# Delta stage's opening: the gate projection over four array quarters with its weights held, and the first convolutions between the normalizations

## The chip, the cores and the metric

One NeuronCore of a Trainium2 chip runs the whole program. The metric is the device time of one execution in microseconds. The profiled execution is another one, taken with the hardware profiler on.

## What is computed

The kernel is a decoder of two layers with six sub-layers (A to F): delta attention, cross attention, a mixture of experts with two choices, local attention, cross attention, and a mixture of 32 experts. Each adds to x. The change lies in the first, A, whose reference begins so (B = 2 sequences of T = 1024 tokens, 256 features, H = 4 heads, NH = 2 key steps a token):

```python
q = short_conv(hidden_states @ Wq, wq_conv).reshape(B, T, H, DK)
k = short_conv(hidden_states @ Wk, wk_conv).reshape(B, T, NH, H, DK)
v = short_conv(hidden_states @ Wv, wv_conv).reshape(B, T, NH, H, DV)
q = l2norm(q)
k = l2norm(k)
beta = 2.0 * jax.nn.sigmoid(hidden_states @ Wb).reshape(B, T, NH, H)
g = -jnp.exp(A_log) * jax.nn.softplus(hidden_states @ Wa + dt_bias)
```

hidden_states is the layer-normalized x; short_conv is a causal convolution over 4 tokens for each channel, and silu. Behind it comes a recurrence over the tokens, which the kernel does in 32 chunks of 32 tokens.

## The kernel before

Every engine runs its own queue in order, and a list `order`, written out in `stage_a`, sets for all of them in which order the steps stand. Each engine's function walks the list and issues its part of a step; semaphores tie the parts together. A step that waits holds everything behind it on its engine.

The steps of the opening:

- **stat, norm, ln** (eight times, for pairs of token tiles in the order `halves`): statistics on DVE (L262, L265), the root on POOL (L284 and `newton`), the normalization on DVE (L275), four transposes on PE (L296), a copy into `XT` on ACT (L304). DVE does stat i two turns ahead of norm i.
- **z**: the projection to the twelve gate columns (Wb and Wa) on PE, L594. Tokens are the stationary operand: 64 matmuls (two passes each) hold 64 tokens and move 12 columns.
- **gates 0, 1, 2**: the gates on DVE and ACT, with small matmuls between 1 and 2 (L604 to L610). **rows** turns the summed decays and sends them to memory (`decays`, `grown`), from where they come back spread over all partitions into `a_E` and `KQg`.
- **conv n, c** (here n = 0, the first 128 tokens, 16 channel tiles c): matmuls on PE (L582, two of 128x256), two copies on ACT (L929, L930), three multiply-adds on DVE (L782). The banks 2, 3, 4 and 7 are taken in turn. On all three engines it waits until `w_in` counts all eight loads of the stage, which SP issues behind x and the constants. **silu** is on ACT (L949), with a small copy on POOL (L1043).
- **kt, sq, root, small, decay**: transposes and norms of the keys, then the decay matrices. From ("kt", 0, 0) on, the chain over the chunks begins.

The order before puts all eight normalizations first, then z and gates 0, then the convolutions:

```python
order += [("z",), ("gates", 0)] + conv0[0:4] + [("gates", 1)] + conv0[4:7] + [("gates", 2), ("rows",)] + conv0[7:11] + silu0[0:4]
```

Of the kernel before, what the change touches and what calls it, by code (L numbers as in the profile page):

```python
# [14 lines left out]
ACT = mybir.ActivationFunctionType  # L15
AX = mybir.AxisListType.X

P = 128
B, T, D = 2, 1024, 256
NT = B * T // P  # L20
TB = T // P
KD = D // P
# [6 lines left out]
R = P // B  # L29
# [109 lines left out]
def program(nc, a, out, stages="ABCDEF"):  # L139
    _, at, _, _ = constant_arrays()  # L140
    with ExitStack() as ctx:
# [20 lines left out]
        XT = sb("XT", [P, KD, B * T])  # L162
# [4 lines left out]
        ident, ones = const("ident"), const("ones")  # L167
# [139 lines left out]
        def stage_a(sx):  # L307
            t_ = lambda name, shape, dt=F32: sb("a_" + name, shape, dt, ctx=sx)
            wqkv, lo = weight_view("a_wqkv", wa, 0)
            wba, lo = weight_view("a_wba", wa, lo)  # L310
# [50 lines left out]
            CP = NC // 2  # L361
            spare_e = E[1][:].rearrange("p a h r -> p (a h r)")
            z = spare_e[:, 0:192].rearrange("p (c n) -> p c n", n=12)
            za, g = (spare_e[:, q:q + CP * H].rearrange("p (c h) -> p c h", h=H) for q in (192, 256))
            n0, n1 = (spare_e[:, q:q + NC * H].rearrange("p (e c h) -> p e c h", e=2, h=H) for q in (384, 512))
# [31 lines left out]
            conv0 = [("conv", 0, q) for q in tiles]  # L397
            silu0 = [("silu", 0, q) for q in tiles]
            halves = [0, 4, 1, 5, 2, 6, 3, 7]
            order = []  # L400
            for i in range(len(halves) + 2):
                order += [("stat", "A", n2) for n2 in halves[i:i + 1]]
                order += [(what, "A", halves[i - 2]) for what in ("norm", "ln")] * (i > 1)
            order += [("z",), ("gates", 0)] + conv0[0:4] + [("gates", 1)] + conv0[4:7] + [("gates", 2), ("rows",)] + conv0[7:11] + silu0[0:4]
            for i in range(11, NCH):
# [51 lines left out]
            at = {}  # L457
            for s in order:
# [6 lines left out]
                elif what == "silu":  # L465
                    silu_done.mark(*s[1:])
                    if s[1] < NB - 1:
                        history.mark(s[1] + 1, s[2])
                elif what == "z":
                    i = 5  # L470
                elif what == "gates":
# [96 lines left out]
            def tensor(t):  # L568
                for s in order:
# [15 lines left out]
                    elif what == "z":  # L585
# [3 lines left out]
                        free(t, *s)  # L589
                        for c in range(CP):  # L590
                            for j in range(KD):
                                for bb in range(B):
                                    first = bb * T + c * R
                                    i = t.e.matmul(b.ap[both(bb), c * 12:c * 12 + 12], XT[:, j, first:first + R], wba[:, j, :],  # L594
                                                   start=j == 0, stop=j == KD - 1, tile_position=(0, bb * R), skip_group_check=True)
                        i.then_inc(b.filled, 1)
# [170 lines left out]
            def vector(v):  # L767
                par = const("par")
                for s in order:
# [18 lines left out]
                    elif what == "gates":  # L788
                        beta, zz = z[:, :, 0:2 * H], z[:, :, 2 * H:3 * H]
                        over = lambda x: x[:, :].unsqueeze(1).broadcast_to([P, CP, H])  # L790
                        if s[1] == 0:
                            zb = at["z",]
                            v.wait_ge(w_in, 128)
                            filled(v, "z")
                            v.e.tensor_copy(z, zb.ap[:, 0:192].rearrange("p (u n) -> p u n", n=12)).then_inc(zb.emptied, 1)
                            emptied(v, "z")
                            v.step(v.e.tensor_tensor(zz, zz, over(dtb), ALU.add)); v.settle()
# [117 lines left out]
            def scalar(c):  # L915
                fence(c, "A")
                for s in order:
# [13 lines left out]
                    elif what == "silu":  # L931
# [16 lines left out]
                        for bb in range(B):  # L948
                            i = c.e.activation(dst[:, :, bb, :], acc_[:, :, bb, :], ACT.Silu)  # L949
                        i.then_inc(silu_done.sem, 1)  # L950
                    elif what == "gates" and s[1] == 0:
                        beta = z[:, :, 0:2 * H]
# [1855 lines left out]
def lay_out(i):  # L2808
# [3 lines left out]
    o["a_wqkv"] = np.concatenate([i["L0_attn_Wq"], i["L0_attn_Wk"], i["L0_attn_Wv"]], 1)  # L2812
    o["a_wba"] = np.concatenate([i["L0_attn_Wb"], i["L0_attn_Wa"]], 1)
    o["a_wg"], o["a_wo"] = i["L0_attn_Wg"], i["L0_attn_Wo"]
# [50 lines left out]
```

## Time and profile before

| what | before |
|---|---|
| median of three runs | 2614.67 us (2614.16 to 2616.9) |
| the profiled execution's own time | 2616.09 us |
| its span | 2614.3 us |
| PE busy | 2287.6 us, 88% |
| DVE busy | 1641.1 us, 63% |
| ACT busy | 1163.2 us, 44% |
| mean granted clock | 0.941 |

Busy time is that of the whole program; the opening spoken of here is its first 77 us. A "pass" is one matmul instruction of the trace; a 32-bit matmul of the code is two of them. Names as `a_kn` are the program's buffers.

### The profile page before, as it was taken

The page shows a single profiled execution, that of the slowest core. Times are in us where ns is not written, and L with a number is a line of the kernel's source. Part 1 is how long each engine was busy: PE and PEld are TensorE (multiplying, and loading weights), DVE is VectorE, ACT ScalarE, POOL GpSimd, SP SyncE. Part 2 cuts the span into 40 slices and gives each one's busy share as a digit, 9 for nine tenths or more (in the row PEclk, how much of TensorE's full clock was granted, in tenths as well). Part 3 has the DMA queues.
Part 4 walks back from the last instruction along what each step waited for, and adds up shares of the span by engine and source line. Part 5 has one row for each costly group of instructions (what it writes and reads, how often), then busy time and mean ns, then how long its engine had stood idle before and what let it go on. Part 6 is the DMA issues. An engine that isn't in the chain of part 4 may idle for free. (4 is left out here: it accounts for less than half of the span.)

```text
span 2614.3 us, 62054 instructions
## 1 busy us (share of the span) xinstructions
PE 2287.6 (88%) x25731; PEld 1873.6 (72%) x25731; DVE 1641.1 (63%) x3593; ACT 1163.2 (44%) x3232; POOL 735.1 (28%) x876
## 2 busy tenths in 40 slices
PE   5689989999898999964998589988887799999998
PEld 4477777777785777743887366666665688888887
DVE  4566676667644555546784455556775767767776
ACT  2544444443423554521554356656775233333332
POOL 2334243423323333331565433420011001111110
PEclk8699999999999999976999799999998899999999
DMA  3101010100103000020442300000000000000000
GB/s 100 57 10 35 27 35 10 35 27 13 61 3 108 9 18 13 13 82 17 114 124 34 103 2 2 2 2 2 2 2 14 13 25 25 25 25 25 25 7 33
DMA packets 87961, 83.35 MB, mean 32 GB/s; under 512 B 27264, under 2 KB 83456, under 8 KB 86272
## 3 DMA queue, kind: packets, MB, share of 16 engines
q1 hardware_dynamic: 81536, 70.98, 8.7%
q0 software_dynamic: 6144, 8.39, 1.9%
q8 instruction: 204, 3.34, 0.5%
q14 instruction: 77, 0.63, 0.1%
HBM read 68.71 MB, written 10.65 MB: 30 GB/s over the span
## 5 line engine op out<-in xcount | busy, mean ns | idle before, releaser
L2566 PE MATMUL bank<-f_XH,f_wp 128*128 128x512 f32 x1088 | 365.4, 397 | 5.9 <-issue 4.5
L782 DVE SCALAR_TENSOR_TENSOR a_acc<-a_praw,a_convw,a_acc 128x256 f32<-128x256 f32 x345 | 205.4, 596 | 99.4 <-ACT a_acc L930 91.2
L2566 PEld LDWEIGHTS bank<-f_XH,f_wp 128*128 128x128 f32 x1088 | 209.1, 192 | 48.5 <-issue 4.9
L2566 PEld LDWEIGHTS bank<-f_wp,f_Hp 128*128 128x128 f32 x1632 | 215.0, 192 | 28.6 <-DVE X L2703 17.0
L2566 PE MATMUL bank<-f_wp,f_Hp 128*128 128x256 f32 x1632 | 219.3, 284 | 17.2 <-DVE X L2703 16.3
L2566 PE MATMUL bank<-f_XL,f_wp 128*128 128x512 f32 x544 | 216.6, 398 | 0.0
L2701 DVE SCALAR_TENSOR_TENSOR X<-bank,f_w,X 128x256 f32<-128x256 f32 x512 | 211.4, 476 | 0.0
L2750 POOL TENSOR_TENSOR f_wp<-wa,f_wp 128x768 fp32r<-128x768 f32 x34 | 62.8, 1848 | 526.2 <-ACT f_wp L2716 526.2
L2739 ACT ACTIVATE f_Hp<-f_H 128x512 fp32r<-128x512 f32 x136 | 85.9, 632 | 225.9 <-DVE f_H L2688 225.9
L582 PE MATMUL bank<-XT,wa 128*128 128x256 f32 x512 | 160.5, 446 | 7.6 <-ACT a_acc L930 6.6
L2737 ACT ACTIVATE f_G<-bank 128x512 f32<-128x512 f32 x136 | 81.3, 598 | 166.0 <-PE bank L2566 166.0
L2690 DVE TENSOR_TENSOR f_Hp<-f_H,f_Hp 128x512 fp32r<-128x512 f32 x136 | 94.2, 692 | 94.9 <-ACT f_Hp L2739 94.9
L669 PE MATMUL bank<-wa 64*64 64x64 f32 x2560 | 108.5, 230 | 46.4 <-DVE wa L871 32.8
L2688 DVE TENSOR_TENSOR f_H<-bank,f_G 128x512 f32<-128x512 f32 x136 | 94.0, 692 | 82.1 <-PE bank L2566 82.1
L2044 DVE TENSOR_REDUCE d_mx<-bank 128x2 f32<-128x512 f32 (+1 forms) x128 | 75.2, 650 | 106.6 <-PE bank L1979 106.6
L669 PEld LDWEIGHTS bank<-wa 64*64 64x64 f32 x2560 | 89.6, 140 | 70.6 <-DVE wa L871 43.6
L997 ACT ACTIVATE wa<-bank 128x256 f32<-128x256 f32 x160 | 58.4, 386 | 159.5 <-PE bank L669 158.7
L1395 POOL TENSOR_TENSOR b_P<-b_P,b_rec 128x616 f32<-128x616 f32 x64 | 77.6, 1212 | 182.9 <-DVE b_rec L1333 182.9
L2114 ACT ACTIVATE d_P<-bank,d_mx 128x256 f32<-128x256 f32 (+1 forms) x256 | 95.1, 479 | 74.6 <-DVE d_mx L2044 74.6
L582 PEld LDWEIGHTS bank<-XT,wa 128*128 128x128 f32 x512 | 100.0, 215 | 28.3 <-ACT a_acc L930 8.9
L2566 PEld LDWEIGHTS bank<-f_XL,f_wp 128*128 128x128 f32 x544 | 104.8, 193 | 16.9
L2432 ACT ACTIVATE e_P<-e_P,e_mx 128x154 f32<-128x154 f32 x256 | 90.7, 415 | 50.2 <-DVE e_mx L2383 50.2
(370 smaller groups left out, 5439.2 us busy)
## 6 DMA issues: line engine op xcount, KB each, us to landing
wa<-in_c_w SPq DMA_DIRECT2D x64, 256.0 KB, 3.3
wa<-in_f_gu SPq DMA_DIRECT2D x34, 256.0 KB, 2.8
wb<-grown SPq DMA_DIRECT2D x4, 1536.0 KB, 6.8
a_KQg<-grown SPq DMA_DIRECT2D x4, 1536.0 KB, 6.6
wa<-in_f_d SPq DMA_DIRECT2D x34, 128.0 KB, 2.9
a_E<-decays SPq DMA_DIRECT2D x16, 256.0 KB, 4.0
X<-in_x SPq DMA_DIRECT2D x4, 512.0 KB, 5.3
wa<-in_a_wqkv SPq DMA_DIRECT2D x1, 2048.0 KB, 11.9
```

The lines of the kernel that those rows point to most:

```text
L582: i = t.e.matmul(b.ap[:, 0:B * BT_].rearrange("p (b t) -> p b t", b=B), wqkv[:, j, c * P:(c + 1) * P], xt, start=j == 0, stop=j == KD - 1, ...
L669: i = t.e.matmul(heads(b.ap)[both(bb), h, :], nt[c % 2][both(bb), h, :], xx[c % 2][both(bb), 0, h, :], start=True, stop=True, tile_positio ...
L782: i = v.e.scalar_tensor_tensor(A_, praw[:, c, :, j:j + BT_], convw[:, c, j:j + 1], A_, ALU.mult, ALU.add)
L1395: g.e.tensor_tensor(p_, p_, bc(rec[:, u % NPB].rearrange("p a b -> p (a b)"), S2), ALU.mult).then_inc(scaled.sem, 1)
L2114: i = c.e.activation(Pm[of(g, r)][:, j, lo:], pair(b.ap)[:, j, lo:], ACT.Exp, bias=mx[:, of(g, r), j:j + 1])
L2432: i = c.e.activation(p_[:, j, :], p_[:, j, :], ACT.Exp, bias=mx[:, of(g, r), j:j + 1])
L2566: i = t.e.matmul(out_, lhsT[x], rhs[y], start=n == 0 and k == 0, stop=n == 2 and k == nk - 1, skip_group_check=True)
L2688: v.e.tensor_tensor(hid[i][:, :], up.ap, gate[i][:, :], ALU.mult).then_inc(up.emptied, 1)
L2690: v.e.tensor_tensor(hp[i][:, 1], hid[i][:, :], whole(hp[i][:, 0]), ALU.subtract).then_inc(parts_ready.sem, 1)
L2701: i = v.e.scalar_tensor_tensor(X[:, n, :], part, w_[:, n, e_:e_ + 1], X[:, n, :], ALU.mult, ALU.add)
L2737: c.e.activation(gate[i][:, :], b.ap, ACT.Silu).then_inc(b.emptied, 1)
L2739: c.e.activation(hp[i][:, 0], hid[i][:, :], ACT.Copy).then_inc(high_ready.sem, 1)
```

## The change

It does four things. z is turned round: the weights (padded from 12 to 32 columns in memory) are stationary and the tokens move, in four groups of 512 tokens, each in 32 columns of the array, so that the result is gates by tokens. ACT copies it into `ST`, a spare part of `a_E`, and a new step **zt** turns it back by four transposes; DVE then copies it out of a differently laid bank. The first six convolutions go between the normalizations, one behind each from the third on. The seventh goes between z and zt, and the others are spread anew over the gate steps; two silus go ahead of gates 2.

```diff
@@ -400,8 +401,9 @@
             for i in range(len(halves) + 2):
                 order += [("stat", "A", n2) for n2 in halves[i:i + 1]]
-                order += [(what, "A", halves[i - 2]) for what in ("norm", "ln")] * (i > 1)
-            order += [("z",), ("gates", 0)] + conv0[0:4] + [("gates", 1)] + conv0[4:7] + [("gates", 2), ("rows",)] + conv0[7:11] + silu0[0:4]
+                order += [(what, "A", halves[i - 2]) for what in ("norm", "ln")] * (i > 1) + conv0[i - 4:i - 3] * (i > 3)
+            order += [("z",)] + conv0[6:7] + [("zt",), ("gates", 0)] + conv0[7:9] + [("gates", 1)] + conv0[9:11] + silu0[0:2]
+            order += [("gates", 2), ("rows",)] + silu0[2:4]
             for i in range(11, NCH):
                 order += [conv0[i]] + silu0[2 * i - 18:2 * i - 16]
...
@@ -587,12 +589,18 @@
-                        for c in range(CP):
-                            for j in range(KD):
-                                for bb in range(B):
-                                    first = bb * T + c * R
-                                    i = t.e.matmul(b.ap[both(bb), c * 12:c * 12 + 12], XT[:, j, first:first + R], wba[:, j, :],
-                                                   start=j == 0, stop=j == KD - 1, tile_position=(0, bb * R), skip_group_check=True)
+                        for j in range(KD):
+                            by_chunk = XT[:, j, :].rearrange("p (b c r) -> p c b r", b=B, r=R)
+                            for q in range(4):
+                                out_ = b.ap[32 * q:32 * q + 32, :].rearrange("p (c b r) -> p c b r", b=B, r=R)
+                                i = t.e.matmul(out_, wba[:, j, :], by_chunk[:, 4 * q:4 * q + 4], start=j == 0, stop=j == KD - 1,
+                                               tile_position=(0, 32 * q), skip_group_check=True)
+                        i.then_inc(b.filled, 1)
+                    elif what == "zt":
+                        emptied(t, "z")
+                        free(t, *s)
+                        for k in range(4):
+                            i = t.e.transpose(b.ap[:, k * P:(k + 1) * P], ST[:, k * P:(k + 1) * P], ident)
                         i.then_inc(b.filled, 1)
...
@@ -789,11 +797,12 @@
-                            filled(v, "z")
-                            v.e.tensor_copy(z, zb.ap[:, 0:192].rearrange("p (u n) -> p u n", n=12)).then_inc(zb.emptied, 1)
-                            emptied(v, "z")
+                            filled(v, "zt")
+                            v.e.tensor_copy(z.rearrange("p (q k) n -> p q k n", q=4),
+                                            zb.ap.rearrange("p (k q n) -> p q k n", k=4, q=4)[:, :, :, 0:12]).then_inc(zb.emptied, 1)
+                            emptied(v, "zt")
...
@@ -948,6 +957,9 @@
+                    elif what == "z":
+                        filled(c, *s)
+                        c.e.activation(ST, b.ap, ACT.Copy).then_inc(b.emptied, 1)
...
@@ -2810,7 +2822,7 @@
-    o["a_wba"] = np.concatenate([i["L0_attn_Wb"], i["L0_attn_Wa"]], 1)
+    o["a_wba"] = np.pad(np.concatenate([i["L0_attn_Wb"], i["L0_attn_Wa"]], 1), ((0, 0), (0, 20)))
```

The queue of DVE before, from the eighth stat on (L262 and L265 are a stat, L275 the norms, L795 to L798 gates 0, L782 convolutions, three rows each):

```order
L262 BN_STATS stats<-X 128x6 x2
L265 BN_AGGR mv<-stats 128x2 x2
L275 TENSOR_SCALAR xn<-X,mv,rs 128x256 x6
L795 COPY a_E<-bank 128x192
L797 TENSOR_TENSOR a_E<-a_E,a_dtb 128x16x4
L798 SCALAR_TENSOR_TENSOR a_E<-a_E 128x64
L782 SCALAR_TENSOR_TENSOR a_kn<-a_praw,a_convw,a_kn 128x256 x12
L801 TENSOR_SCALAR a_E<-a_E 128x16x8
```

The same queue of the changed kernel, from the third norm on. The lines of the file have moved by 8 (L790 is the convolution):

```order
L275 TENSOR_SCALAR xn<-X,mv,rs 128x256 x2
L790 SCALAR_TENSOR_TENSOR a_kn<-a_praw,a_convw,a_kn 128x256 x3
L262 BN_STATS stats<-X 128x6 x2
L265 BN_AGGR mv<-stats 128x2 x2
L275 TENSOR_SCALAR xn<-X,mv,rs 128x256 x2
L790 SCALAR_TENSOR_TENSOR a_kn<-a_praw,a_convw,a_kn 128x256 x3
```

A convolution's three operations now stand ahead of the next stat and norm; before, none stood ahead of the last norm.

The queue of PE before, up to the first projections (L296 transposes of the normalization, L594 z, L582 projection):

```order
L296 MATMUL bank<-wide,xn 128x128 x32
L594 MATMUL bank<-wa,XT 64x12 x64
L582 MATMUL bank<-XT,wa 128x256 x8
L604 MATMUL bank<-a_E,wide 128x128
L606 MATMUL bank<-a_E,wide 128x64
L604 MATMUL bank<-a_E,wide 128x128
```

And of the changed kernel, from the first transposes up to those of zt (L584 projection, L596 z, L603 zt):

```order
L296 MATMUL bank<-wide,xn 128x128 x12
L584 MATMUL bank<-XT,wa 128x256 x2
L296 MATMUL bank<-wide,xn 128x128 x4
L584 MATMUL bank<-XT,wa 128x256 x2
L296 MATMUL bank<-wide,xn 128x128 x4
...
L296 MATMUL bank<-wide,xn 128x128 x4
L584 MATMUL bank<-XT,wa 128x256 x2
L596 MATMUL bank<-XT,wa 32x512 x8
L584 MATMUL bank<-XT,wa 128x256 x2
L603 MATMUL bank<-wide,a_E 128x128 x4
```

Each projection stands behind the four transposes of a normalization and ahead of those of the next; z is 8 matmuls instead of 64, and one projection lies between it and the new transposes.

## Rows read from the trace of the kernel before

**Rows 1.** The page of the profile, its first line.

```profile
span 2614.3 us, 62054 instructions
```

**Rows 2.** Timeline: start us, duration us, engine, line, operation; end of the opening.

```profile
68.84 7.27 DVE L782 SCALAR_TENSOR_TENSOR a_kn<-a_praw,a_convw,a_kn 128x256 f32<-128x256 f32 x15 [1.55 <-ACT a_kn L930]
...
87.32 0.17 DVE L822 TENSOR_SCALAR a_kss<-a_kss 128x16 f32<-128x16 f32 x1 [11.21 <-ACT a_junk L988]
```

**Rows 3.** Stretches, L582 alone: PE busy and passes, weight loads, granted clock, DMA.

```profile
34.00:39.00 5.00, 4.95 (x12) 3.98 (x13) 1.00 0.00 2
...
60.00:63.00 3.00, 3.00 (x8) 2.37 (x8) 0.50 0.18 55
...
63.00:67.00 4.00, 4.00 (x19) 3.48 (x18) 0.98 0.96 223
```

**Rows 4.** Timeline, queue of SP: the last of the stage's loads is issued.

```profile
18.95 0.43 SPq L548 DMA_DIRECT2D a_onw<-in_a_onw  x1
```

**Rows 5.** DMA issues: KB each, median us from issue to landing.

```profile
a_onw<-in_a_onw SPq DMA_DIRECT2D x1, 32.0 KB, 3.2
...
a_E<-decays SPq DMA_DIRECT2D x2, 256.0 KB, 4.2
```

**Rows 6.** Timeline, one normalization before: DVE stat and norm, PE transposes.

```profile
15.20 0.74 DVE L262 BATCH_NORM_STATS2 stats<-X 128x6 f32<-128x256 f32 x2
...
16.14 0.70 DVE L275 TENSOR_SCALAR xn<-X,mv,rs 128x256 f32<-128x256 f32 x2
...
16.89 1.11 PE L296 MATMUL bank<-wide,xn 128*128 128x128 f32 x4 [0.45 <-DVE xn L275]
```

**Rows 7.** Timeline, one convolution in its steps, lower clock.

```profile
60.34 0.38 ACT L929 ACTIVATE a_praw<-bank 128x256 f32<-128x256 f32 x1 [1.01 <-PE bank L582]
...
61.12 1.53 DVE L782 SCALAR_TENSOR_TENSOR a_kn<-a_praw,a_convw,a_kn 128x256 f32<-128x256 f32 x3 [3.06 <-ACT a_kn L930]
...
83.01 1.12 PE L622 MATMUL bank<-wide,wb 128*128 128x128 f32 x4 [2.90 <-ACT a_kn L979]
...
83.92 1.92 PE L582 MATMUL bank<-XT,wa 128*128 128x256 f32 x4
...
87.96 2.07 PE L582 MATMUL bank<-XT,wa 128*128 128x256 f32 x4 [2.13 <-ACT a_acc L930]
...
90.16 0.38 ACT L929 ACTIVATE a_praw<-bank 128x256 f32<-128x256 f32 x1 [2.24 <-PE bank L582]
```

**Rows 8.** Timeline, the gate steps before.

```profile
43.67 0.22 DVE L801 TENSOR_SCALAR a_E<-a_E 128x128 f32<-128x128 f32 x1
...
45.33 0.79 PE L604 MATMUL bank<-a_E,wide 128*128 128x128 f32 x2 [4.99 <-DVE a_E L804]
...
48.80 4.86 PE L582 MATMUL bank<-XT,wa 128*128 128x256 f32 x12
...
56.22 0.28 DVE L808 COPY a_G<-bank 128x128 f32<-128x128 f32 x1
...
58.10 0.45 ACT L962 ACTIVATE a_GCe<-bank 128x128 f32<-128x128 f32 x2 [2.36 <-DVE a_eKd L818]
```

**Rows 9.** Timeline, the gate projection before and what follows it.

```profile
27.11 7.01 PE L594 MATMUL bank<-wa,XT 128*64 128x12 f32 x128 [0.78 <-ACT XT L304]
...
34.22 0.36 DVE L795 COPY a_E<-bank 128x192 f32<-128x192 f32 x1 [9.06 <-PE bank L594]
...
37.16 0.37 ACT L929 ACTIVATE a_praw<-bank 128x256 f32<-128x256 f32 x1
```

**Rows 10.** Timeline, stage C's logits: the same form in four column groups.

```profile
1154.82 3.64 PE L1608 MATMUL bank<-XT,c_wg 128*32 128x512 f32 x16 [0.84 <-ACT XT L304]
...
1158.52 0.60 ACT L1780 ACTIVATE c_ST<-bank 128x512 f32<-128x512 f32 x1
```

**Rows 11.** Timeline, one convolution's matmuls and copy, upper clock.

```profile
102.45 1.13 PE L582 MATMUL bank<-XT,wa 128*128 128x256 f32 x4 [0.30 <-ACT a_acc L930]
...
103.70 0.38 ACT L929 ACTIVATE a_praw<-bank 128x256 f32<-128x256 f32 x1 [0.90 <-PE bank L582]
```

More of the change, by code:

```diff
@@ L363, in stage_a @@
             z = spare_e[:, 0:192].rearrange("p (c n) -> p c n", n=12)
+            ST = spare_e[:, 512:1024]
             za, g = (spare_e[:, q:q + CP * H].rearrange("p (c h) -> p c h", h=H) for q in (192, 256))
@@ L468, in stage_a @@
                         history.mark(s[1] + 1, s[2])
-                elif what == "z":
-                    i = 5
+                elif what in ("z", "zt"):
+                    i = 5 if what == "zt" else 6
                 elif what == "gates":
@@ L791, in vector @@
                         if s[1] == 0:
-                            zb = at["z",]
+                            zb = at["zt",]
                             v.wait_ge(w_in, 128)
-                            filled(v, "z")
-                            v.e.tensor_copy(z, zb.ap[:, 0:192].rearrange("p (u n) -> p u n", n=12)).then_inc(zb.emptied, 1)
-                            emptied(v, "z")
+                            filled(v, "zt")
+                            v.e.tensor_copy(z.rearrange("p (q k) n -> p q k n", q=4),
+                                            zb.ap.rearrange("p (k q n) -> p q k n", k=4, q=4)[:, :, :, 0:12]).then_inc(zb.emptied, 1)
+                            emptied(v, "zt")
                             v.step(v.e.tensor_tensor(zz, zz, over(dtb), ALU.add)); v.settle()
```

## Prediction

> **What bounds the kernel now.** I read the page first: one core, span 2614.3 us [rows 1]. The change touches only the opening of the first stage (delta attention), about the first 77 us. So the first question is whether a microsecond there is a microsecond of the whole. In order of time, DVE ends the last of the sixteen first convolutions at 68.84 + 7.27 = 76.11; ACT follows with the last silus and goes straight over to the next steps ("kt", "sq"), and DVE stands idle for 11.21 us, up to 87.32, for ACT's squares [rows 2]. Everything behind is a serial chain (norms of the keys, decays, chunks). I find no transfer or other work in it that would absorb a shift. I therefore count the whole change as the shift of that 76.11, which both orders have: the steps from ("kt", 0, 0) on are the same.
>
> Next, the opening. Its matmuls run at the lower clock for most of it. Twelve passes of the projection (L582, two passes a matmul, 256 columns) took 34 to 39 us, 0.41 us each. That is the pace of the stretch at a granted clock of 0.50 (8 in 3 us), and not that of the stretch at 0.98 (19 in 4 us) [rows 3]. The 1.00 written beside the first stretch is thus not the pace: up to 39 us TensorE works at its 1.2 GHz level. It rises only behind a long unbroken run of matmuls.
>
> **The start of the new order.** The convolutions wait on w_in for all eight of the stage's loads. The last of them, a_onw, is issued at 18.95 [rows 4] and lands 3.2 us later [rows 5]: 22.15. Before, nobody saw this; the first waiter was z at 27.11, behind all eight normalizations. Now conv 0 stands in the queues of PE, ACT and DVE behind the third of eight normalizations, and DVE would reach it at about 15.2, when the statistics of the sixth pair used to start [rows 6]. Queued behind it on DVE are stat 5 to 7 and norm 3 to 7, and for each norm wait PE and ACT. All of that stands still until 22.15, and about 3 us longer, for conv 0 must be computed and copied: matmuls to ACT's copy 90.16 - 87.96 = 2.20, ACT to DVE 61.12 - 60.34 = 0.78 [rows 7]. Conv 0 on DVE: 22.15 + 2.98 = 25.1.
>
> **The loop.** From there one normalization and one convolution alternate, and the queues tie them into one ring. DVE must finish conv k before it does stat and norm; PE has the transposes of that norm ahead of the matmuls of conv k+1; ACT copies; DVE needs the copy before conv k+1. One turn: three DVE operations 1.53 (I take 1.50 to the next start), stat to norm 16.14 - 15.20 = 0.94, norm to PE 16.89 - 16.14 = 0.75 [rows 6], transposes to matmuls 83.92 - 83.01 = 0.91, then 2.20 and 0.78 [rows 7]: 7.08 us, or 6.14 without a stat. PE is busy for some 2.6 us of a turn, so I see nothing to raise its clock. Conv 1 to 5 are three turns with and two without a stat: 33.5 us. Conv 5 starts on DVE at 58.6. By then the old order had finished 8 normalizations, z, both gate steps and seven convolutions: gates 2 started at 56.22 [rows 8].
>
> **z.** Removed: 64 matmuls in 128 passes, 34.22 - 27.11 = 7.11 us to DVE's copy [rows 9]. Added: 8 matmuls of 128x512 into four column groups, the very form that stage C runs as its logits: 16 passes, ACT's copy 1158.52 - 1154.82 = 3.70 us behind the first, at the lower clock (one pass alone is busy 1.06) [rows 10]. Gain 3.4. The Trainium skill, TensorEngine Tiling (Array Packing), "Theoretical Speedup", gives up to 4x for a dimension of at most 32. Taken against today's z this would be 7.11 / 4 = 1.8 and the sum 1.9 us lower; the row shows 1.9x, because the old form moved only 12 columns a pass, and I use the row. Added behind it: ACT's copy into ST, 0.7 with its wait; then four transposes, 1.2 with theirs [rows 7], which wait on PE behind conv 6. These take back 1.9 and more.
>
> **From conv 5 to the end, at the lower clock.** Its matmuls began at 55.6 and occupy PE 4 x 0.43, so z starts at 57.3 and fills at 61.0. Conv 6 lies ahead of the transposes on PE and its DVE work ahead of gates 0: gates 0 on DVE at 65.3. From there to ACT's first conv copy 37.16 - 34.22 = 2.94 [rows 9], to DVE 0.78: 69.0; two convolutions 3.0; gates 1 on DVE to PE 45.33 - 43.67 = 1.66, PE to the next projection 48.80 - 45.33 = 3.47 [rows 8]: 77.1. Then 2.98 to DVE, two convolutions 3.2: gates 2 at 83.3; 58.10 - 56.22 = 1.88 [rows 8] brings ACT to the exponents at 85.2. ACT now loads a table twice more, as silu is put on both sides of them: a load, two silus and 1.3 of exponents, conv 11 reaches DVE at 89.3. Five convolutions at ACT's pace of 1.6: 97.2. So at the lower clock all through the shift is 97.2 - 76.1 = 21.1 us.
>
> Two stretches should be faster. z, conv 6, the transposes, conv 7 and 8 fill PE for some 9 us on end, as do the gate matmuls with conv 9 and 10 for 6. At the upper clock matmuls to copy take 103.70 - 102.45 = 1.25 instead of 2.20 [rows 11]. I take off 1.3 and 1.7. **Sum: 97.2 - 3.0 - 76.1 = +18 us.**
>
> Bounds. Upper: +21 as above. Lower: everything at the upper clock. A turn is then 1.50 + 0.94 + 0.75 + 0.45 + 1.25 + 0.78 = 5.67, or 4.73; five are 26.5 instead of 33.5, and the part from conv 5 on 34.9 instead of 38.6. With 0.95 at conv 0: 85.6, +9.5 us. Unpriced: the strided moving operand of z (64 elements in a run; the projection's is in two pieces and costs nothing), a_wba with 32 instead of 12 columns (20 KB more), PE's and DVE's waits themselves. I put each at 0 to 0.5 us. The decays leave for memory about 26 us later too, but their load took 4.2 us [rows 5], some 8 with the store ahead of it, and POOL is free for them only when it has copied the last convolution's tail, at about 94. That work is the cover; without it the cost would be a few us more.
>
> The profiled execution took 2616.09 us, 1.8 more than its span and 1.4 more than the median of the runs, 2614.67. The forecast is 2614.67 + 18 = 2632.7.
>
> **Rivals.**
> 1. *The ring turns at the upper clock*, in part or in whole: +9.5 to +13, 2624 to 2628. For it: transposes and matmuls in every turn keep PE from long idleness. Against it: from 60 to 63 us the clock stood at 0.50 with PE busy throughout [rows 3], and a turn has it busy for 2.6 us of 7.
> 2. *A part is absorbed later* (a wait of chunk 0 for the grown rows or for POOL, which I read as not binding): +5 to +9, 2620 to 2624. Against it: DVE waits for nothing but ACT there [rows 2].
> 3. *Faster: DVE is the bound.* If the waits of the opening were filled by convolutions that run ahead, DVE's own work would set the end: from 25.1, five norms and three stats 6, sixteen convolutions 23.4, gates 4.4, end 58.9, shift -17, 2597.5. This needs PE and ACT to have conv k+1 ready when DVE ends conv k. The point from which it decides: the end must fall below 76.1 - 5.2 = 70.9, that is 23 us under my sum. The five turns hold 33.5 us, of which DVE's own work is 13.4; all their waiting taken away gives 20, so the ring alone can't do it, the gates would have to overlap too.
> 4. *No change*: the shorter z pays for the ring. It would need the ring to cost 3 us; a turn of about 3.5 instead of 7.
>
> **Chances.** What the measurement can tell is about 0.2%, 5.2 us. Forecast (+13 to +22) 0.68; rival 1 0.16; rival 2 0.06; rival 4 0.05; rival 3 0.05. Slower 0.90, same 0.05, faster 0.05. The range takes the forecast and rival 1: 2624 to 2637.
>
> **What the profile after would show.** DVE idle from about 15.3 to 25 us behind a wait on w_in and ACT; conv 0 to 5 on DVE at distances of 7.1, 7.1, 7.1, 6.1, 6.1 us; the last transposes of the first normalizations at about 55 instead of 25.2 us; z of 16 passes in 3.6 us; gates 0 on DVE at about 64; the exponents for the decays at about 82; the last first convolution done at 94 instead of 76.1, and the step behind it (POOL's root) the same 18 us later. Wrong would be a ring of 3 to 4 us (then the DVE order allows more than I read), or a shift at 76 us that is gone at 107.

## The result, and the profile after

| | before | after |
|---|---|---|
| median of 7 runs each, alternating on one chip | 2616.9 us (2614.16 to 2623.94) | 2635.68 us (2625.04 to 2639.13) |
| profiled execution / its span | 2616.09 / 2614.3 us | 2639.13 / 2637.3 us |
| start of DVE's root step, behind the opening | 87.32 us [rows 2] | 104.58 us |

The changed kernel is slower: its time is 1.0067 of before's, 95% interval 1.0047 to 1.0086, or 17.5 us (12 to 22). The forecast was +18 us.

The first lines of the page after, to be held against [rows 1]:

```profile
span 2637.3 us, 61840 instructions
```

Timeline after, the first convolution and the first two turns behind it (start, duration, engine, line; in brackets the idle time before, and what ended it). L584 is the projection, L938 and L939 ACT's two copies of it, L790 the convolution on DVE, L596 z, L603 the turn back, L803 gates 0:

```profile
21.91 2.08 PE L584 MATMUL bank<-XT,wa 128*128 128x256 f32 x4 [5.69 <-DMA a_onw<-in_a_onw]
24.10 0.39 ACT L938 ACTIVATE a_praw<-bank 128x256 f32<-128x256 f32 x1 [7.25 <-PE bank L584]
24.95 1.53 DVE L790 SCALAR_TENSOR_TENSOR a_kn<-a_praw,a_convw,a_kn 128x256 f32<-128x256 f32 x3 [9.90 <-ACT a_kn L939]
26.40 0.74 DVE L262 BATCH_NORM_STATS2 stats<-X 128x6 f32<-128x256 f32 x2
27.34 0.70 DVE L275 TENSOR_SCALAR xn<-X,mv,rs 128x256 f32<-128x256 f32 x2
28.10 1.11 PE L296 MATMUL bank<-wide,xn 128*128 128x128 f32 x4 [4.12 <-DVE xn L275]
29.01 1.91 PE L584 MATMUL bank<-XT,wa 128*128 128x256 f32 x4
30.96 0.39 ACT L938 ACTIVATE a_praw<-bank 128x256 f32<-128x256 f32 x1 [1.11 <-PE bank L584]
31.74 1.53 DVE L790 SCALAR_TENSOR_TENSOR a_kn<-a_praw,a_convw,a_kn 128x256 f32<-128x256 f32 x3 [3.70 <-ACT a_kn L939]
...
38.53 1.52 DVE L790 SCALAR_TENSOR_TENSOR a_kn<-a_praw,a_convw,a_kn 128x256 f32<-128x256 f32 x3 [3.70 <-ACT a_kn L939]
...
45.32 1.52 DVE L790 SCALAR_TENSOR_TENSOR a_kn<-a_praw,a_convw,a_kn 128x256 f32<-128x256 f32 x3 [3.70 <-ACT a_kn L939]
...
47.55 0.66 PE L296 MATMUL bank<-wide,xn 128*128 128x128 f32 x4 [3.05 <-DVE xn L275]
...
50.61 1.53 DVE L790 SCALAR_TENSOR_TENSOR a_kn<-a_praw,a_convw,a_kn 128x256 f32<-128x256 f32 x3 [3.12 <-ACT a_kn L939]
...
55.59 3.32 PE L596 MATMUL bank<-XT,wa 128*32 128x512 f32 x16
...
56.48 1.53 DVE L790 SCALAR_TENSOR_TENSOR a_kn<-a_praw,a_convw,a_kn 128x256 f32<-128x256 f32 x3 [3.69 <-ACT a_kn L939]
58.84 1.13 PE L584 MATMUL bank<-XT,wa 128*128 128x256 f32 x4
...
62.23 0.35 DVE L803 COPY a_E<-bank 128x192 f32<-128x192 f32 x1
```

Read the rows from 24.95 to 31.74 as one turn of the ring. DVE convolves, then does the stat and the norm (26.40, 27.34); PE transposes that norm (28.10) and only then projects (29.01); ACT copies (30.96); DVE convolves again. Each bracket names the engine before it in the ring. The six convolutions stand 6.79, 6.79, 6.79, 5.29 and 5.87 us apart.

The same timeline, further on, to be held against [rows 2, 8]:

```profile
68.80 0.22 DVE L810 TENSOR_SCALAR a_E<-a_E 128x128 f32<-128x128 f32 x1
70.45 0.79 PE L612 MATMUL bank<-a_E,wide 128*128 128x128 f32 x2 [8.32 <-DVE a_E L813]
73.92 3.73 PE L584 MATMUL bank<-XT,wa 128*128 128x256 f32 x8
79.91 0.28 DVE L817 COPY a_G<-bank 128x128 f32<-128x128 f32 x1
...
86.09 7.27 DVE L790 SCALAR_TENSOR_TENSOR a_kn<-a_praw,a_convw,a_kn 128x256 f32<-128x256 f32 x15 [4.34 <-ACT a_kn L939]
...
104.58 0.17 DVE L831 TENSOR_SCALAR a_kss<-a_kss 128x16 f32<-128x16 f32 x1 [11.21 <-ACT a_junk L1000]
```

The last convolution is done at 86.09 + 7.27 = 93.36 us, 17.25 later than the 76.11 of before, and the root step is 17.26 later: the wait of 11.21 between them is the same. In what follows this root step, DVE's L831 (L822 before), is the marker of the opening's end: 87.32 before, 104.58 after.

The waits of DVE from 0 to 97 us, after (us in total, times, longest):

```profile
DVE a_kn L790 <- ACT a_kn L939: 37.8, 9, 9.9
DVE a_acc L790 <- ACT a_acc L939: 6.5, 2, 6.4
```

And before, where the same wait had L782 and L930, and DVE waited for z as well:

```profile
DVE a_kn L782 <- ACT a_kn L930: 14.0, 5, 6.4
DVE a_E L795 <- PE bank L594: 9.1, 1, 9.1
```

DVE waits 37.8 + 6.5 = 44.3 us for ACT's copies where it waited 14.2 (14.0 for a_kn and one wait of 0.2 for a_acc; up to 97 us in both, which takes in 10 us more of what follows before's root step), and no longer 9.1 for z.

In this one pair of profiles the spans differ by 23.0 us, and only 17.3 are at the marker. Line by line the shift is 19.2 at the end of the delta stage, 21.6 at stage C's logits and 21 to 25 from there on. Medians say 17.5 to 18.8. The profiled execution was the slowest of the seven, and the mean granted clock of its core was 0.930 against before's 0.941; runs of one kernel lie up to 14 us apart here. I count the 17.3 as the change's; that the rest is this spread is argued and not shown.

### The profile page after: what moved, and what is told of

The parts are those of the page before. It is cut to its first block and busy times, and to the rows that moved or that the text cites. A ratio compares the mean times of both kernels' runs of the same rounds, so it can differ in the third digit from the quotient of the medians.

```text
span 2637.3 us, 61840 instructions
## 1 busy us (share of the span) xinstructions
PE 2300.2 (87%) x25623; PEld 1878.1 (71%) x25623; DVE 1640.1 (62%) x3593; ACT 1166.2 (44%) x3234; POOL 735.3 (28%) x876
## 5 line engine op out<-in xcount | busy, mean ns | idle before, releaser
L790 DVE SCALAR_TENSOR_TENSOR a_acc<-a_praw,a_convw,a_acc 128x256 f32<-128x256 f32 x345 | 205.3, 595 | 105.5 <-ACT a_acc L939 97.2
L584 PE MATMUL bank<-XT,wa 128*128 128x256 f32 x512 | 164.0, 451 | 12.1 <-ACT a_acc L939 6.3
L1009 ACT ACTIVATE wa<-bank 128x256 f32<-128x256 f32 x160 | 58.6, 387 | 159.9 <-PE bank L677 159.1
L584 PEld LDWEIGHTS bank<-XT,wa 128*128 128x128 f32 x512 | 100.1, 216 | 33.6 <-ACT a_acc L939 8.7
L284 POOL TENSOR_SCALAR rs<-mv 128x2 f32<-128x2 f32 x48 | 12.0, 250 | 370.0 <-DVE mv L265 368.7
```

Source lines behind the costliest of these rows:

```text
L584: i = t.e.matmul(b.ap[:, 0:B * BT_].rearrange("p (b t) -> p b t", b=B), wqkv[:, j, c * P:(c + 1) * P], xt, start=j == 0, stop=j == KD - 1, ...
L790: i = v.e.scalar_tensor_tensor(A_, praw[:, c, :, j:j + BT_], convw[:, c, j:j + 1], A_, ALU.mult, ALU.add)
```

## The experiments

Each was timed in five rounds beside the kernel before. "Marker" is the start of DVE's root step in the experiment's profile. The table is for reference; the reading follows one by one. The fourth column is (ratio - 1) x 2616.

| kernel | marker | against before's 87.32 | whole, us | ratio, 95% interval |
|---|---|---|---|---|
| after | 104.58 | +17.3 | +17.5 | 1.0067 [1.0047, 1.0086] |
| e1 z turned, alone | 87.25 | -0.1 | -2.1 | 0.9992 [0.9983, 1.0002] |
| e2 ring, alone | 107.20 | +19.9 | +22.8 | 1.0087 [1.0071, 1.0103] |
| e3 ring cut on DVE | 81.70 | -5.6 | -5.2 | 0.9980 [0.9968, 0.9992] |
| e4 loads awaited apart | 100.14 | +12.8 | +16.7 | 1.0064 [1.0048, 1.0079] |
| e5 e3 and e4 | 82.12 | -5.2 | -6.5 | 0.9975 [0.9962, 0.9988] |
| e6 before, DVE delayed | 100.99 | +13.7 | +14.1 | 1.0054 [1.0038, 1.0071] |
| e7 gates respaced | 72.72 | -14.6 | -8.9 | 0.9966 [0.9953, 0.9978] |
| e8 PE kept busy in the ring | 99.61 | +12.3 | +19.1 | 1.0073 [1.0059, 1.0086] |
| e9 e7, delayed | 85.77 | -1.6 | -3.7 | 0.9986 [0.9975, 0.9998] |
| e10 e7 with the old z | 72.78 | -14.5 | -17.0 | 0.9935 [0.9918, 0.9951] |
| e11 e7 once more | 72.36 | -15.0 | -14.7 | 0.9944 [0.9925, 0.9964] |
| e12 e10 once more | 73.45 | -13.9 | -14.9 | 0.9943 [0.9927, 0.9960] |

**e1: z turned, all else in before's order.** Conv 0 alone goes between z and zt.

```diff
-                order += ... + conv0[i - 4:i - 3] * (i > 3)
-            order += [("z",)] + conv0[6:7] + [("zt",), ("gates", 0)] + conv0[7:9] + [("gates", 1)] + conv0[9:11] + silu0[0:2]
+            order += [("z",)] + conv0[0:1] + [("zt",), ("gates", 0)] + conv0[1:4] + [("gates", 1)] + conv0[4:7]
...
```

> The turned gate projection alone: all eight normalizations first again, then z, conv 0, zt, gates 0 and the rest in the order of before. Marker: the start of DVE's step root (87.32 us before, 104.58 after). Theory (the ring of normalization and convolution costs everything): z to its copy 3.7 instead of 7.1 us, of which ACT's copy, the transposes and conv 0 in front of them take back most; the marker at 84 to 87, the whole 0 to 4 us faster than before. Rival (the turned projection with its extra hop from PE to ACT and back is what costs): marker above 95, the whole at least 8 us slower than before.

Timeline of e1, z and what follows:

```profile
27.16 3.64 PE L596 MATMUL bank<-XT,wa 128*32 128x512 f32 x16 [0.78 <-ACT XT L304]
30.73 2.08 PE L584 MATMUL bank<-XT,wa 128*128 128x256 f32 x4
...
32.60 0.66 PE L603 MATMUL bank<-wide,a_E 128*128 128x128 f32 x4
...
33.78 1.52 DVE L790 SCALAR_TENSOR_TENSOR a_kn<-a_praw,a_convw,a_kn 128x256 f32<-128x256 f32 x3 [8.56 <-ACT a_kn L939]
35.22 0.35 DVE L803 COPY a_E<-bank 128x192 f32<-128x192 f32 x1
```

z takes 3.64 us instead of 7.01 [rows 9], but gates 0 start at 35.22, not at 34.22: conv 0 stands ahead of the transposes on PE and ahead of gates 0 on DVE. Conv 0 is then done, so gates 1 start at 43.23 instead of 43.67 [rows 8]. Of these 0.44 us, 0.07 are left at the marker. (The unbroken run of 32 passes behind gates 2 starts 0.40 us earlier than before's, at 57.99, and takes 0.33 longer, 9.77 against 9.44: the clock does not rise with it.) The turned z is worth nothing that the measurement can tell.

**e2: the ring alone.** The new order with the old z, and so without zt; the cut shows its line of the order against after's.

```diff
-            order += [("z",)] + conv0[6:7] + [("zt",), ("gates", 0)] + ...
+            order += [("z",)] + conv0[6:7] + [("gates", 0)] + ...
```

> The new places of the convolutions with the old gate projection (64 matmuls, no zt). Theory: the ring and the gate steps pushed behind it are untouched, and z is some 3 us dearer less the removed hop: marker at 104 to 108, the whole 17 to 21 us slower than before. Rival (the turned projection costs): marker near 90, the whole within 5 us of before.

The marker is 19.9 us late and the whole 1.0087: the new order costs all of the loss and some more (I had expected 17 to 21 us of the whole; 22.8 is a little above). Against e2, after is 2.6 earlier at the marker; 0.8 of that stood already at conv 5 (57.27 against 56.48), ahead of z, and is the pace of a turn. About 1.8 are left for the turned z in this order. Timeline of e2, DVE:

```profile
45.53 1.53 DVE L783 SCALAR_TENSOR_TENSOR a_kn<-a_praw,a_convw,a_kn 128x256 f32<-128x256 f32 x3 [3.70 <-ACT a_kn L931]
...
51.40 1.52 DVE L783 SCALAR_TENSOR_TENSOR a_kn<-a_praw,a_convw,a_kn 128x256 f32<-128x256 f32 x3 [3.69 <-ACT a_kn L931]
...
57.27 1.52 DVE L783 SCALAR_TENSOR_TENSOR a_kn<-a_praw,a_convw,a_kn 128x256 f32<-128x256 f32 x3 [3.70 <-ACT a_kn L931]
```

Here both turns without a stat take 5.87; the 5.29 of after's fourth turn was one at the upper clock (its transposes took 0.66 instead of 1.11).

**e3: the ring cut at DVE alone.** PE and ACT keep after's order; DVE takes convolutions 0 to 5 behind its last norm.

```diff
+            early = conv0[0:6]
+            dve_order = [s for s in order if s not in early]
+            behind = dve_order.index(("norm", "A", halves[-1])) + 1
+            dve_order[behind:behind] = early
...
-                for s in order:
+                for s in dve_order:
```

> The changed kernel with one edit: DVE's part of conv 0 to 5 stands behind the last norm in DVE's queue; PE and ACT keep the new order. Theory (the cost is the ring through DVE's queue): the normalizations no longer wait for convolutions on DVE, PE does transposes and projections back to back from 22 us, and the marker comes to 82 to 88, the whole -5 to +1 us against before, that is 17 to 22 us less than the changed kernel. Rival (the cost is the wait for the loads and the slow clock of a PE that starts late): marker 98 to 105, at most 6 us better than the changed kernel.

Timeline of e3 (L795 is the convolution, L589 the projection):

```profile
21.73 2.07 PE L589 MATMUL bank<-XT,wa 128*128 128x256 f32 x4 [5.42 <-DMA a_onw<-in_a_onw]
...
25.88 1.03 PE L589 MATMUL bank<-XT,wa 128*128 128x256 f32 x4
...
29.28 10.15 DVE L795 SCALAR_TENSOR_TENSOR a_kn<-a_praw,a_convw,a_kn 128x256 f32<-128x256 f32 x21
...
30.93 1.92 PE L601 MATMUL bank<-XT,wa 128*32 128x512 f32 x16
```

Seven convolutions run on DVE without a wait, 1.45 us each, where five turns took 31.5. PE still waits for a_onw, projects between the same transposes, and is then at the upper clock. Moving nothing but DVE's six steps takes the marker from 104.58 to 81.70 and turns a loss of 17.5 us into a gain of 5.2. It is the closed ring that costs, not the projections' place on PE. The loads still cost something here: PE and, as e5 will show, POOL wait for a_onw, and the last norm is at 28.63 where before's was at 24.43.

**e4: the loads awaited apart.** The projection waits for w_qkv and the convolution's weights on a semaphore of their own, loaded first.

```diff
-                for name, view in (("a_wqkv", wqkv), ("a_wba", wba), ...
-                    y.e.dma_start(view, by_rows(name)).then_inc(w_in, 16)
+                y.e.dma_start(wqkv, by_rows("a_wqkv")).then_inc(conv_in, 16)
+                y.e.dma_start(convw[:, :, :], ...).then_inc(conv_in, 16)
+                for name, view in (("a_wba", wba), ("a_wg", wg), ("a_wo", wo)):
...
-                        t.wait_ge(w_in, 128)
+                        t.wait_ge(conv_in, 32)
```

> The changed kernel with the ring kept, but the convolutions wait only for the projection weights and the convolution weights, which are the first two loads of the stage on a semaphore of their own. Theory: conv 0 starts on PE at about 17 instead of 21.9 us and the ring runs on at the same 6.8 and 5.3 us a turn: marker 5 us earlier, at 99 to 100, the whole 11 to 13 us slower than before. Rival (waiting for the loads is the main cost): marker below 92, the whole within 5 us of before.

Timeline of e4:

```profile
17.93 2.08 PE L585 MATMUL bank<-XT,wa 128*128 128x256 f32 x4 [1.56 <-DMA a_convw<-in_a_conv]
...
20.98 1.53 DVE L791 SCALAR_TENSOR_TENSOR a_kn<-a_praw,a_convw,a_kn 128x256 f32<-128x256 f32 x3 [5.78 <-ACT a_kn L940]
```

Conv 0 comes 3.97 us earlier and the marker 4.4. So of the 17.3 about 4 are the wait for eight loads and 13 are the turns and what stands behind them. The whole, 1.0064, does not stand apart from after's 1.0067: at this size the medians don't tell. I had expected a whole of 11 to 13 us above before; 16.7 is above that, and within its interval.

**e5: e3 and e4 together.**

```diff
+            early = conv0[0:6]
+            dve_order = [s for s in order if s not in early]
...
-                        t.wait_ge(w_in, 128)
+                        t.wait_ge(conv_in, 32)
```

> e3 and e4 together: DVE's part of conv 0 to 5 behind the last norm, and the convolutions wait only for the two loads they need. Theory (two prices that add: the ring, and the wait for the loads with everything queued behind it): marker (start of root on DVE, 87.3 before, 81.7 in e3) 4 us earlier than in e3, at 77 to 79; the whole 8 to 12 us faster than before. Rival (with the ring cut the wait for the loads is hidden, DVE or the gate steps bind): marker above 80.5, the whole as e3.

The marker stays at 82.12, as the rival had it. Timeline of e5, DVE and POOL:

```profile
22.89 0.22 POOL L284 TENSOR_SCALAR rs<-mv 128x2 f32<-128x2 f32 x1 [4.34 <-DMA a_onw<-in_a_onw]
...
25.11 0.74 DVE L275 TENSOR_SCALAR xn<-X,mv,rs 128x256 f32<-128x256 f32 x2 [4.78 <-POOL rs L221]
...
27.31 0.73 DVE L275 TENSOR_SCALAR xn<-X,mv,rs 128x256 f32<-128x256 f32 x2 [1.46 <-POOL rs L221]
```

Without the ring, the last norms wait for POOL's roots, 2.2 us a pair (25.11 to 27.31). And POOL had itself waited 4.34 us for a_onw. A convolution's step waits for the loads not on three engines but on four: POOL's queue has the same wait, ahead of the roots of the last three pairs, and this edit left it on the other six loads:

```diff
-                    g_.wait_ge(w_in, 128)
+                    g_.wait_ge(w_in, 96)
```

So e5 moved the wait for the loads from PE, ACT and DVE to POOL and did not remove it: the last norm is at 29.51, against 24.43 in before, and the convolutions begin behind it, at 30.16 here and 29.28 in e3. Whether the price of the loads adds to that of the ring, as I had expected, is therefore not tested. e7 and e9 to e12 have the same wait (POOL starts again at 22.06 in e7, the last norm is at 28.69). Without it the convolutions could begin up to some 4 us earlier, an estimate from 28.69 - 24.43 that no run here tries.

**e6: the kernel before with DVE held up.** It adds 70 statistics that nothing reads ahead of gates 0.

```diff
+                            for n in range(70):
+                                v.step(v.e.bn_stats(stats[:, n % NT, :], X[:, n % NT, :]))
```

> The kernel before with nothing but a delay: 70 statistics operations on DVE, whose result nobody reads, ahead of gates 0, about 26 us of which DVE idled 9 anyway. It asks whether a microsecond at the end of the opening is one of the whole. Theory (it is; what differs beyond it between executions is the clock of later stages): marker 16 to 18 us later, at 103 to 106, the whole 14 to 21 us slower than before. Rival (later waits absorb a part): the whole 5 us or more short of the marker's shift. Second rival (a delay costs more than itself, since it leaves TensorE colder): the whole 5 us or more above it.

They took 0.33 us each, less than I had reckoned, so the marker moves by 13.7; the whole moves by 14.1 (10 to 18 by its interval). Within some 4 us, a shift of the opening passes to the end one for one, as the prediction had it.

**e7: DVE's order respaced.** On top of e5, gates 0 stand behind four convolutions, gates 1 behind three more, gates 2 behind four more; PE and ACT project 7 to 10 ahead of gates 1's matmuls.

```diff
+            order += [("z",)] + conv0[6:7] + [("zt",), ("gates", 0)] + conv0[7:11] + [("gates", 1), ("gates", 2), ("rows",)] + silu0[0:4]
...
+            turn_of = conv0[0:4] + [("gates", 0)] + conv0[4:7] + [("gates", 1)] + conv0[7:11] + [("gates", 2)]
```

> e5, and the gate steps placed by DVE's time: gates 0 behind conv 3, gates 1 behind conv 6, gates 2 behind conv 10, with the projections of conv 7 to 10 ahead of the gate matmuls on PE and ACT. Theory (in e3 DVE idles some 12 us around gates 1 and 2 because the convolutions that could fill it stand behind the gate matmuls on PE): marker at 69 to 74, the whole 13 to 18 us faster than before. Rival (the decays' trip to memory then ends last, or ACT binds): marker above 76, at most 3 us better than e5.

Timeline of e7, DVE:

```profile
29.34 5.83 DVE L795 SCALAR_TENSOR_TENSOR a_kn<-a_praw,a_convw,a_kn 128x256 f32<-128x256 f32 x12
35.09 0.35 DVE L808 COPY a_E<-bank 128x192 f32<-128x192 f32 x1
...
35.88 4.39 DVE L795 SCALAR_TENSOR_TENSOR a_kn<-a_praw,a_convw,a_kn 128x256 f32<-128x256 f32 x9
40.19 0.22 DVE L815 TENSOR_SCALAR a_E<-a_E 128x128 f32<-128x128 f32 x1
...
47.45 0.28 DVE L822 COPY a_G<-bank 128x128 f32<-128x128 f32 x1
...
54.23 7.28 DVE L795 SCALAR_TENSOR_TENSOR a_kn<-a_praw,a_convw,a_kn 128x256 f32<-128x256 f32 x15 [4.94 <-ACT a_kn L944]
```

DVE has no wait from 29.34 up to the end of gates 2, and the marker is at 72.72, 14.6 us ahead of before. But the whole was only 8.9 us faster, where I had expected 13 to 18: a miss, taken up by e9 to e12.

**e8: the ring with PE kept busy.** Four matmuls into a bank that nothing reads go behind each of the six projections.

```diff
+                        if s in conv0[0:6]:
+                            for _ in range(4):
+                                t.e.matmul(banks[5].ap[:, 0:B * BT_]..., wqkv[:, j, c * P:(c + 1) * P], xt, start=True, stop=True, ...)
```

> The changed kernel, ring and all, with four more 128x256 matmuls into an unread bank behind each of the projections of conv 0 to 5, which fill PE's idle part of a turn. It asks how much of a turn is the clock. Theory (a turn is 7.1 us at the lower clock and 5.7 at the upper; both far above the 3.7 that a normalization and a convolution took apart from each other): the clock rises within two or three turns, the later turns take 5.5 to 6 and 4.6 to 5.2 us, marker 100 to 103, still 11 to 16 us slower than before. Rival (the slow clock is the main cost of the ring): marker below 95. If the fillers themselves delay the transposes: marker at or above 104.6.

Timeline of e8, the projections of the first two turns:

```profile
28.73 1.03 PE L584 MATMUL bank<-XT,wa 128*128 128x256 f32 x4
...
34.30 1.91 PE L584 MATMUL bank<-XT,wa 128*128 128x256 f32 x4
```

The turns shrink to 5.49, 6.46, 5.49, 4.56 and 4.58 us and the marker comes 5.0 us earlier than after's, although PE does more work: at least that much of the ring is the lower clock's share. The second turn shows the lower level again, its projection at 1.91 us where the first had 1.03. The median did not follow (1.0073), the profiled execution did (its span is 2626.8, 10.5 less than after's). I hold the reading of the turns for shown and that of the whole for open.

**e9: e7 with DVE held up ahead of the marker** by 39 statistics that nothing reads, 13.1 us. It asks whether e7's missing microseconds come back when its later stages start when before's do.

```diff
+                        for k in range(0 if n else 39):
+                            v.step(v.e.bn_stats(stats[:, k % NT, :], X[:, k % NT, :]))
```

> e7 with 39 unread statistics operations, about 14.6 us, on DVE ahead of root 0, behind the end of the opening, so that the first chunk starts when it does before. e7's first chunk started 14.4 us early, but its median was only some 9 us faster. Theory (the missing part is the clock of the chunks, which differs from execution to execution and has nothing to do with when the opening ends): the first chunk within 1 us of before, the whole within 5 us of before. Rival (e7's order itself leaves something dearer behind it, 5 to 6 us in the chunks): the whole 5 to 7 us slower than before. Second rival (an earlier start meets a wait later that absorbs a part): the whole within 2 us of before, exactly what the delay takes back being less than 14.6.

**e10: e7 with the old z,** 64 matmuls and no zt.

```diff
-            order += [("z",)] + conv0[6:7] + [("zt",), ("gates", 0)] + conv0[7:11] + ...
+            order += [("z",)] + conv0[6:7] + [("gates", 0)] + conv0[7:11] + ...
```

> e7 with the old gate projection: 64 matmuls that hold tokens, no ST copy and no transposes. It asks what the turned projection is worth once the queues let it pay. Theory (at the upper clock z turned is 1.9 us, the old one of 128 passes bound by its weight loads some 3.5 us, or 7 if the clock falls in it; the hop over ACT and PE takes 1.5 to 2 back, and gates 0 stands behind conv 3 on DVE): marker 0 to 4 us later than in e7, at 73 to 77, the whole 0 to 4 us slower than e7. Rival (with the ring cut the turned projection is the source of e7's gain): marker above 82.

e9 and e10 were timed on one chip, beside the same runs of before. Their markers are 85.77 - 72.78 = 12.99 us apart and their ratios 0.0051, or 13.3 us: one for one again (the two differ in z as well, for which e11 and e12 show no price). e9 itself, with a marker 1.6 us ahead of before's, is 3.7 us faster (0.5 to 6.5), so at most some 1 us is lost behind the marker. e10 has e7's marker within 0.06 us and yet came out 8 us faster than e7, timed on another chip. Either the turned z costs something in later stages, or one of the two figures is off by more than its interval says.

**e11 and e12: e7 and e10 once more, on one chip,** unchanged.

> The kernel of e7_gates_respaced once more, timed beside the respaced kernel with the old z, on the same chip. In their first runs, on different chips, these two ended the opening at the same time (DVE's root step at 72.72 and 72.78 us) and differed by 0.0031 in their ratios to the kernel before, about 8 us. Theory: the opening's end sets the time, and the turned z is worth nothing either way, so the two come out within 4 us of each other here and both between 8 and 17 us faster than before (ratios 0.9935 to 0.997). Rival: the turned z costs the later stages some 8 us by a way that the opening doesn't show; then this one stays at 0.9966 and the other at 0.9935, with intervals that don't meet.

> The kernel of e10_respaced_old_z once more, beside the respaced kernel with the turned z. Theory: within 4 us of that one, ratio 0.9935 to 0.997. Rival: 8 us faster than that one, ratio 0.9935 against 0.9966.

Timeline of e12, the old z at the upper clock for most of its passes:

```profile
31.24 4.46 PE L600 MATMUL bank<-wa,XT 128*64 128x12 f32 x128
```

0.9944 and 0.9943: side by side the two are 0.3 us apart by their ratios and 3.1 by their medians (2603.33 and 2600.2), less than an interval, and both are as much faster as their markers are earlier (15.0 and 13.9). The turned z is worth nothing that these runs can tell in this order. The same kernel, timed on two chips, gave 0.9966 and 0.9944, with intervals that overlap; as e11 fits its marker and e7 does not, I take e7's 8.9 for the figure that was off. So a ratio over five rounds is here to be trusted to about 0.2%, which is what the prediction took. The best version, 0.9935 to 0.9966 over its four timings, is DVE's order respaced, with either z.

## Why the prediction was right

*The opening's shift is the whole's.* Held: root step +17.26, whole +17.5, and e6 moved the one by 13.7 and the other by 14.1. In the table, whole and marker agree within 4 us for eleven of the thirteen rows, within 7 for e7 and e8.

*Start.* Conv 0 on DVE was forecast for 25.1 and came at 24.95; PE's wait is named a_onw, 5.69 us, and e4 gives the price of that wait: 4.4 us at the marker.

*The loop.* The ring of DVE, PE and ACT is what the rows show, and e3, which opens it at one link, removes it with the whole loss. The size of a turn was 0.29 too large: 7.08 against 6.79. Two terms of it were mis-sized. The 2.20 from matmuls to ACT's copy [rows 7] was read from a projection that began behind idle time (2.08 us busy); behind the transposes it is 1.91 busy, and 30.96 - 29.01 = 1.95 to the copy. DVE's 1.50 was 1.45. The fourth turn had part of the upper clock besides (5.29 against 5.87 of the fifth). Five turns took 31.53 us, not 33.5. The prediction saw nothing in a turn that would raise the clock, and wrote that it rises only behind a long unbroken run of matmuls; the fourth turn is against both, for its transposes took 0.66 us behind 3.05 us of idle time. That four of the five turns ran at the lower level is what kept the forecast near.

*z.* Forecast 3.70 to ACT's copy, measured 58.98 - 55.59 = 3.39, and its last passes already neared the upper clock: conv 6's matmuls behind it took 1.13. e1 has it at the lower clock throughout: 3.64 us against 7.01, 1.9x. e3 and e10 have both forms at the upper one, 1.92 against 3.91, 2.0x; e10's row is this:

```profile
30.98 3.91 PE L600 MATMUL bank<-wa,XT 128*64 128x12 f32 x128
```

The Trainium skill, TensorEngine Tiling (Array Packing), "Theoretical Speedup", gives up to 4x for a dimension of at most 32; an estimate by it is 7.01 / 4 = 1.8 us for z at the lower clock. No run here shows more than 2.0x over the old form, and taking the row rather than the page was right.

*From conv 5 to the end.* Forecast 94.2 - 58.6 = 35.6 us, measured 93.36 - 56.48 = 36.88. Up to gates 0 it was 5.75 against 5.4. Between gates 1 and gates 2 it was 79.91 - 68.80 = 11.11 where I had 11.3 less 1.7 for the upper clock. That 1.7 did not come: behind 8.32 us of idle time and 3.5 us of gate matmuls the eight passes at 73.92 took 3.73 us, the pace of 1.2 GHz. The last piece was 13.45 against 13.9. The two larger errors, 1.97 too long in the ring and 1.5 too short here, nearly cancel; the sum, +18 against +17.25 at the last convolution, is better than its terms, and that much of it is luck.

*The rivals.* Rival 1 (the ring at the upper clock, +9.5 to +13) did not happen by itself; e8 shows that a busy PE would have brought the marker down to +12.3. Rival 2 (9 to 13 us absorbed later) is ruled out by e6, which lost at most some 4 of 13.7. Rival 4 needed a turn of 3.5 us. Rival 3, DVE as the bound, with its -17 us, is not what this change does, but it is what e7 and e10 to e12 come near, by opening the ring *and* overlapping the gates, as the prediction said both would be needed: -14 to -15 at the marker.

*Not settled:* why the profile's shift grows from 17.3 to 23 behind the opening in this one execution, and why e8's median did not follow its marker. In seven of the thirteen profiles, e1 and e3 among them, the delta stage behind the marker takes 4 to 5 us longer than in before, in the others from 1 less to 2 more; I found no edit that goes with it.

## What to carry to other kernels

When independent work is woven into a loop that passes through in-order queues, follow one item round all of them: if each engine has the next item's first step behind this item's last, every pass costs the sum of the links, however idle the engines are. Weave on the engines that only feed (here PE and ACT), and let the consumer (DVE) run its own loop to the end before it takes what was woven in; e3 did that with a few lines. And ask what the first woven step waits for: a semaphore shared by all loads is free for a late reader and costs an early one the last of them. Look for that wait in every queue: e5 took it from three and left it on the fourth.

## What I had not expected of the hardware

TensorE's clock in the ring, after, L584 alone in stretches of 3 us (PE busy and passes, weight loads, granted clock, DMA):

```profile
42.00:45.00 3.00, 1.91 (x4) 1.23 (x4) 0.53 0.01 3
45.00:48.00 3.00, 0.00 (x0) 0.06 (x1) 1.00 0.00 0
48.00:51.00 3.00, 1.75 (x4) 0.92 (x4) 0.54 0.00 0
```

In one and the same ring the clock stood at 1.2 GHz in the stretch from 42 us, was granted in full in the next, where the four transposes at 47.55 took 0.66 us instead of 1.11, and was back at the lower level before the four passes from 48 us were done. In e8, with PE busy for 4.7, 4.2, 4.0, 3.2 and 3.3 us of the five turns, the first turn's projection ran in 1.03 us and the second's in 1.91. So even with a steady pattern of work the level is not steady from turn to turn.

And work of PE that nothing needs made the critical path shorter: eight passes of filler in each turn of e8 took 5.0 us off the marker, though the median of the whole did not show it. In e1, the other way about, what was won ahead of the long run of passes was nearly gone behind it.
